# One fp32 output product per context tile in place of three fp16 products

## The reference, cut to what matters

```
c_q, c_kv = h @ w_down_q.T, h @ w_down_kv.T            # rank 64 each
q, k, v   = (c_q @ w_up_q.T), (c_kv @ w_up_k.T), (c_kv @ w_up_v.T)   # 16 heads of 64
scores    = rope(q) @ rope(k).T / 8 ;  attn = softmax(scores)
out       = concat_heads(attn @ v) @ w_out.T + x_normalised
```

## Time and profile before

| | us |
|---|---|
| median of three runs | 1675.15 (1670.72 to 1676.22) |
| the profiled execution | 1674.69 |
| its span, first to last instruction | 1672.9 |
| attention units, one | about 37 |

### The profile page before, as it was taken

One profiled execution on the slowest core, in us unless ns is written; L12 is line 12 of the kernel. 1 busy time (PEld: TensorE's weight loads), 2 busy tenths in 40 slices (PEclk: granted clock), 3 DMA queues, 4 the chain that ended last, 5 costly groups with the idle time before them and its releaser, 6 DMA issues. The chain is left out here.

```text
span 1672.9 us, 47969 instructions
## 1 busy us (share of the span) xinstructions
PE 1560.3 (93%) x19008; PEld 1024.6 (61%) x19008; DVE 1464.2 (88%) x3079; ACT 1215.7 (73%) x1679; POOL 1297.8 (78%) x904
## 2 busy tenths in 40 slices
PE   3899884999999999999999999999999999957999
PEld 2566640566666666666666666666666666635666
DVE  4788887899999999999999999999999998746663
ACT  3333261788888888888888888988888888843442
POOL 1454505799999999999999999999999997723555
PEclk9999985999999999999999999999999999968999
DMA  5333302021111112211111112112111211002333
GB/s 169 95 102 99 104 1 76 12 68 40 40 44 45 49 31 57 51 40 40 49 49 31 50 43 56 40 40 59 30 49 35 64 40 40 2 1 96 116 121 126
DMA packets 65629, 96.17 MB, mean 57 GB/s; under 512 B 11776, under 2 KB 24064, under 8 KB 65152
## 3 DMA queue, kind: packets, MB, share of 16 engines
q1 hardware_dynamic: 62320, 92.18, 20.1%
q10 hardware_dynamic: 3088, 0.92, 0.2%
HBM read 40.24 MB, written 2.36 MB: 25 GB/s over the span
## 5 line engine op out<-in xcount | busy, mean ns | idle before, releaser
L1208 POOL TENSOR_TENSOR area<-area 128x1024 f16<-128x1024 f32 (+1 forms) x512 | 833.8, 1647 | 82.9 <-ACT area L1171 75.8
L1076 DVE TENSOR_REDUCE area<-ps 128x1 f32<-128x512 f32 x1024 | 665.4, 685 | 16.6 <-PE ps L963 12.9
L1169 ACT ACTIVATE area<-ps 128x1024 f16<-128x1024 f32 x512 | 525.6, 1027 | 145.5 <-PE ps L990 145.4
L1007 PE MATMUL ps<-cv_all,area 128*128 128x65 f16 x4096 | 454.9, 193 | 3.3 <-POOL area L1208 3.2
L1009 PE MATMUL ps<-cv_all,area 128*128 128x64 f16 x4096 | 456.8, 195 | 0.0
L1011 PE MATMUL ps<-cv_all,area 128*128 128x65 f16 x4096 | 453.7, 192 | 0.0
L1009 PEld LDWEIGHTS ps<-cv_all,area 128*128 128x128 f16 x4096 | 381.3, 97 | 78.9
L1007 PEld LDWEIGHTS ps<-cv_all,area 128*128 128x128 f16 x4096 | 383.9, 97 | 63.2 <-issue 9.7
L963 PE MATMUL ps<-area 128*128 128x512 f16 x1024 | 393.1, 384 | 13.9 <-DMA area<-area 9.0
L989 PE MATMUL ps<-area 128*128 128x512 f16 x1024 | 388.7, 380 | 1.7 <-DVE area L1105 0.4
L990 PE MATMUL ps<-area 128*128 128x512 f16 x1024 | 389.0, 380 | 0.0
(11 more groups left out here) (156 smaller groups left out, 2271.3 us busy)
## 6 DMA issues: line engine op xcount, KB each, us to landing
area<-area SPq DMA_DIRECT2D x384, 128.0 KB, 2.7
area<-f_w_rows_in_dram SPq DMA_DIRECT2D x128, 256.0 KB, 3.2
xg<-in_x SPq DMA_DIRECT2D x4, 512.0 KB, 7.6
out_x<-xg SPq DMA_DIRECT2D x3, 512.0 KB, 4.4
area<-in_wup SPq DMA_DIRECT2D x1, 1024.0 KB, 7.9
cs<-in_rope SPq DMA_DIRECT2D x1, 1024.0 KB, 8.6
area<-area SPq DMA_DIRECT2D x64, 2.0 KB
area<-in_wo ACTq DMA_DIRECT2D x1, 512.0 KB, 6.7
```

The costliest lines, as they stand in the source:

```text
L1007: nc.tensor.matmul(o, p_hi[:, s % 4, c:c + P], latents[:, 0:DH + 1], start=first, stop=False, skip_group_check=True)
L1076: nc.vector.tensor_reduce(mx[:, hd, kh, qt:qt + 1], bank, AX.X, ALU.max).then_inc(s_mr, 1)
L1169: nc.scalar.activation(p_hi[:, s % 4, :], sc, ACT.Exp, scale=0.125).then_inc(s_e16, 1)
L1208: nc.gpsimd.tensor_tensor(p_lo[:, s % 4, c0:], src[:, (s // 2) % 2, :], p_hi[:, s % 4, c0:], ALU.subtract).then_inc(s_pp, 1)
```

## The change

The transposed context is copied once, in fp32, and wc is kept in fp32; OP makes one fp32 product for each block. `context_low` and `latent_out_low` are gone, and the reads that release the PSUM banks are signalled by the single copy of each.

```diff
-        wc_hi = sb("wc_hi", [P, PAIRS, D], F16)
-        wc_lo = sb("wc_lo", [P, PAIRS, D], F16)
+        wc = sb("wc", [P, PAIRS, D])
...
         def latent_out_high(act):
             act.wait_ge(s_wc, 1)
             for rows, js, bank in wc_parts:
-                nc.scalar.copy(wc_hi[rows, js, :], ps[rows, bank, :].rearrange("p (j d) -> p j d", d=D)).then_inc(s_wch, 1)
-
-        def latent_out_low(v):
-            for n, (rows, js, bank) in enumerate(wc_parts):
-                v.wait_ge(s_wch, n + 1)
-                nc.vector.tensor_tensor(wc_lo[rows, js, :], ps[rows, bank, :].rearrange("p (j d) -> p j d", d=D),
-                                        wc_hi[rows, js, :], ALU.subtract).then_inc(s_wcr, 1)
+                nc.scalar.copy(wc[rows, js, :], ps[rows, bank, :].rearrange("p (j d) -> p j d", d=D)).then_inc(s_wcr, 1)
...
-        cxt_hi = carve(S, F16).rearrange("p (t n) -> p t n", t=TB)
-        cxt_lo = carve(S, F16).rearrange("p (t n) -> p t n", t=TB)
+        cxt = carve(S).rearrange("p (t n) -> p t n", t=TB)
...
                     if first:
-                        latent_out_low(v)
                         for c in (2, 3):
...
-        dve_order = ("aaaL aSCaa TtLm Ttrb bL rbS bPbLbPC bb bbb LbbSb bCcbL ncc rc LcrS cc LCccc").split()
+        dve_order = ("aaaL aSCaa TLm Trb bL rbS bPbLbPC bb bbb LbbSb bCcbL ncc rc LcrS cc LCccc").split()
...
-                        pe.wait_ge(s_oh, u * 2 + (i + 1))
                         pe.wait_ge(s_mr, ot_read[i])
                         for t in range(4):
-                            a = [c_[:, 4 * i + t, :] for c_ in (cxt_hi, cxt_lo)]
-                            for m, (x_, y_) in enumerate(((0, 0), (0, 1), (1, 0))):
-                                last = nc.tensor.matmul(bank[:, P * t:P * t + P], a[x_], (wc_hi, wc_lo)[y_][:, w % PAIRS, :],
-                                                        start=(t == 0 and m == 0), stop=(m == 2), skip_group_check=True)
+                            last = nc.tensor.matmul(bank[:, P * t:P * t + P], cxt[:, 4 * i + t, :], wc[:, w % PAIRS, :], start=(t == 0),
+                                                    stop=True, skip_group_check=True)
...
-                        nc.vector.tensor_copy(cxt_hi[:, c_, :], bank.rearrange("p (t n) -> p t n", t=4)).then_inc(s_oh, 1)
+                        nc.vector.tensor_copy(cxt[:, c_, :], bank.rearrange("p (t n) -> p t n", t=4)).then_inc(s_mr, 1)
...
-                def context_low(item, u, par):
-
-                    i = item[3]
-                    c_ = slice(4 * i, 4 * i + 4)
-                    v.wait_ge(s_oh, u * 2 + (i + 1))
-                    nc.vector.tensor_tensor(cxt_lo[:, c_, :], ps[:, 6 + par, :].rearrange("p (t n) -> p t n", t=4), cxt_hi[:, c_, :],
-                                            ALU.subtract).then_inc(s_mr, 1)
...
-                            elif c == "t":
-                                context_low(converted, u, 1 - par)
...
                     misc(item, UNITS, 0, n + m, (n + m) % 2)
-                    if item[0] == "OT":
-                        context_low(item, UNITS, (n + m) % 2)
```

More of the change, by code:

```diff
@@ L129, in build @@
         s_hi, s_lo, s_wc = sem("w_hi_done"), sem("w_lo_done"), sem("wc_product")
-        s_wch, s_wcr = sem("wc_hi_done"), sem("wc_read")
+        s_wcr = sem("wc_read")
         s_uph, s_upl = sem("up_hi_done"), sem("up_lo_done")
@@ L341, in build @@
         s_pv, s_rs, s_cx = sem("pv"), sem("row_sums_inverted"), sem("context")
-        s_oh = sem("context_T_hi")
         def ffn(name):
@@ L1146, in unit @@
                                     context(*grp)
-                            elif c == "t":
-                                context_low(converted, u, 1 - par)
                             elif todo and todo[0] in of_letter.get(c, ()):
-                                converted = todo.pop(0)
-                                misc(converted, u, k, n, par)
+                                misc(todo.pop(0), u, k, n, par)
                                 n, par = n + 1, 1 - par
```

## The result

The changed kernel takes 1683.2 us (median of six runs, 1682.4 to 1685.1) where the kernel before took 1675.4 beside it. The ratio is 1.0052, with a 95% interval of 1.0039 to 1.0065: slower by half a per cent. (The ratio is that of the means of the runs, so it is not quite 1683.2 / 1675.4.) The profiled execution took 1682.88 us, 8.2 more than the one of before.

What follows compares the result with a forecast made beforehand. PE's queue was taken to bound the kernel. OP's +14.1, +0.2 after the last unit and -3.7 in f1 gave +10.6 us on 1674.69: 1685.3; the forecast's own range was 1681 to 1690, the 8-in-10 range 1675 to 1690.

Steps and rivals of the forecast that it cites:

- PE sets the pace: Attention units: PE's starts add up to 36.69 of 36.96 us, so its queue stands still only 0.27.
- OP costs 0.22 more per item: OP on PE: an item goes from 0.67 to 0.89 us, as four fp32 products make eight matmul records.
- The rival of uncovered weight loads: OP: fp32 weight loads of 0.195 set the pace, 1.56 us an item, time 1730; chance 0.03.
- +14.1: Attention units: OP's two longer items cost +0.44 us per unit, times 32 units.
- The last unit: Last attention unit: OP's delay passes through PE's pauses; at worst it is hidden there, 0.44 us less.
- context_low at nothing inside a unit: DVE sheds 1.4 us per unit; PE's 0.06 before the second OT comes back at L989, so no gain.
- the wait of step 4: Units, step 4: PE's L989 waits for ACT's L1171; 0.06 saved earlier there becomes 0.06 more standing still.
- f1 at -3.7: Start of f1: ACT's copies release PE 4.6 us earlier; with twelve products at half level, gain taken as 3.7.
- After the last unit, +0.2: Behind the last unit: OP starts 0.7 us earlier without the subtraction but ends at 1483.9 instead of 1483.7.
- the stalls go: Rival, units: DVE's relief removes PE's 0.27 of stalls in 31 units, +2.2 us, time 1676.9; chance 0.14.
- DVE sets the pace: Rival, units: each falls by the 1.4 us DVE sheds, 45 us in all, time 1626; chance 0.03.
- one pass: Rival, OP: an fp32 product is one record of 0.11, an item 0.44 us, time 1655.8; chance 0.05.

Runs made afterwards that it cites:

- fp32_twice: Changed kernel with each fp32 product of OP issued twice into the same sum; 1741.5 us, ratio 1.0402.
- the two runs on DVE's relief: no_context_low (DVE's subtractions left out of the kernel before), 1674.8 us; second_read (DVE work put back into the changed kernel), 1684.5 us.
- the short OPs: Changed kernel with wc and context copy in fp16, 1656.3 us; early_release without context_low, high context against both halves of wc, 1659.4 us.
- after_cast: Changed kernel with ACT's cast moved from step 2 to 3 and POOL's low halves from steps 3 and 5 to 4 and 5; 1680.0 us, ratio 1.0034.
- early_cast: early_release with ACT's cast moved from step 2 to 3, POOL's low halves from steps 3 and 5 to 4 and 5; 1666.4 us, ratio 0.9951.
- second_read: Changed kernel with DVE reading the bank again by a subtraction behind each context copy, before the bank's release; 1684.5 us, ratio 1.0065.
- early_release: Kernel before with only f1's start changed: ACT copies wc in fp32 first, releasing PE, then makes the fp16 half; 1669.3 us, ratio 0.9968.
- after_late_release: Changed kernel, but PE's first gate product also waits for four small DVE copies behind the routing work; 1689.2 us, ratio 1.0081.
- no_context_low: Kernel before without DVE's 66 context_low subtractions, OP's third product reading the high half again; 1674.8 us, ratio 1.0002.

## Why the prediction was right, and where its sizes were off

It forecast 1685.3 us (+0.6%) and slower with a chance of 0.76; the time is 1683.2 (+0.5%). Taken by its steps:

- *PE sets the pace* held at the lengths concerned: fp32_twice paid 1.79 for 1.78, and the two runs on DVE's relief moved no unit. It doesn't hold much further down, as the short OPs showed: had the change made OP 0.22 shorter, the same argument would have promised 0.44 a unit, and the unit fell by 0.25.
- *OP costs 0.22 more per item* was 0.22 for the first and 0.27 for the second of a unit. The rival of uncovered weight loads, to which I gave 0.03, is there in small, 0.05 of the 0.67 that it would have cost beyond my 0.22: PE may load for the second OP only once DVE has read the bank, and then 0.06 of cover is left. Twelve fp16 products lost nothing by the same wait; these lines are the second OP of a unit of the kernel before, with 0.05 of lead and 0.67 long like the first:

```profile
835.07 0.10 PEld L978 LDWEIGHTS ps<-wc_hi,area 128*128 128x128 f16 x1
835.12 0.22 PE L978 MATMUL ps<-wc_hi,area 128*128 128x128 f16 x1
...
835.79 0.38 PE L989 MATMUL ps<-area 128*128 128x512 f16 x1
```

  No run was made for this, but the traces show the late load to be the reason. In after_cast the first OP came to 0.07 of lead, and its length went from 0.89 to 0.93. And item by item in the two traces, in us, every bit of lead that is missing comes back as length, all of it between the first record and the second (0.16 where the others are 0.11 apart):

| lead of the first load | 0.028 | 0.054 | 0.060 | 0.066 | 0.214 |
|---|---|---|---|---|---|
| length of the item | 0.971 | 0.943 | 0.937 | 0.931 | 0.891 |

  The units came to +15.5 us in place of +14.1: the late loads are 1.5 of it over 31 units, one unit near the end has a wait of 0.3 more, and the last unit 0.44 less.
- *The last unit* was priced at +0.44 and came out at 0.0 (29.78 before, 29.77 after, between OTs). The chain passes the delay through as I said (fp32_twice adds 1.79 to the last unit too, 31.56); but in the trace of before the clock fell to its half level 2 us ahead of the first OT behind the last unit, inside the last probability products, and in the trace after it did not. The DVE line that waits for these products shows the difference, 1.92 us here and 1.45 in the kernel after:

```profile
1477.58 0.18 DVE L1124 RECIPROCAL area<-ps 128x4 f32<-128x4 f32 x1 [1.92 <-PE ps L1011]
```

- *context_low at nothing inside a unit* was right to the 0.06: it left the second OT, and the wait of step 4 went from 0.21 to 0.27.
- *f1 at -3.7* was -5.1 at the transposes and -5.3 at the first OT. The mechanism was right. I let all twelve products run at the half level, but the clock rose within them, and from 30.55 on they are 0.22 apart: they took 4.23 us and not 5.15, and the transposes 0.6. That is in part luck: in kernels with the same start the clock rose at other times, in early_cast at 31.97 and in second_read at 32.74, where the twelve took 4.90 and 5.08. The first OT of the kernels with the early release comes anywhere from 300.1 to 303.4, so one pair of profiled executions gives this term to a few us only; the medians of early_release (5.4) and after_late_release (4.9) are the better measure.
- *After the last unit, +0.2* was -1.9, the term most wrong, and again by a clock level. I carried the half level over from the trace of before. After, all of it ran at the full level. Of the 1.9, the subtraction and the length of OP account for 0.9 and the level for 1.1: early_cast has the tail of the kernel before at the full level and needs 5.5 us, against 6.6 and the 4.7 of the changed kernel.

The errors by stretch, +1.4 in the units, -1.6 ahead of them and -2.1 behind, partly cancel; that the sum came within 2.4 us of the profiled execution is no evidence for each term.

Among the rivals, "the stalls go" and "DVE sets the pace" were refuted by no_context_low, which takes DVE's work away and leaves the unit as it is, and "one pass" by the eight records in 0.89.

## What to carry to other kernels

When two engines both look nearly full (here PE 36.92 and DVE 35.97 of 36.96 us), add up one engine's starts over a period. Here that sum was all but 0.27 of the period, and it was this engine that paid, while the other's relief was worth nothing. The price holds only in the direction in which you add work: in the other, the next engine takes over, here within the first 0.22 us taken off OP. And of a change that bundles parts, price each alone: here a 5 us gain at the start, which needed no fp32 product, hid a third of a 15 us loss.

## What the runs showed of the hardware

- An fp32 product of 128x128 by 128 columns is two matmul records and 0.223 us of PE's queue at full clock; an fp16 one is one record and 0.056. Three fp16 products from halves, 0.168, are cheaper than one in fp32, but for DVE's second pass over the result, which here was free.
- An fp32 weight load lasts 0.19 us, and the first of an item wants more lead than an fp16 one: with 0.05 us of lead the fp32 item is 0.05 longer, the fp16 one not at all. Lead and length of a late fp32 item add up to 0.995 to 0.999 in all late items of the kernel after and of after_cast (0.028 + 0.971, 0.054 + 0.943, 0.066 + 0.931), against a full length of 0.891; the lead that it needs is by that some 0.106, an estimate.
- A DVE copy from PSUM of 128x512 takes 0.691 us in fp32 and 0.692 when it casts to fp16.
- The clock's fall at the end of attention came 1.6 to 2.3 us before the first OT behind the last unit in some traces and 2.7 to 10.6 after it in others, also between kernels with the same tail (early_release 2.3 before, early_cast 7.7 after). The level there is worth about 1.1 us behind the last unit and 0.5 inside it, and belongs to no part of the change that I can name.
- The clock's first rise in f1 came between 30.2 and 33.0 us in the traces of kernels whose first gate product starts at 27.0 to 27.4, and moved the first OT by up to 3 us.
